# An expert FFN on one Trainium2 core: the first two up products before the last group's counts

## The reference

```python
gate = softmax(flat_x @ w_gate.T)                  # 8 experts
topk_scores, topk_idx = top_k(gate, 2)
cw = (one_hot(topk_idx, 8) * topk_scores[..., None]).sum(axis=1)
h = gelu(einsum('td,edh->teh', flat_x, W1) + b1, approximate=False)   # hidden width 512
y = einsum('teh,ehd->ted', h, W2) + b2
out = einsum('ted,te->td', y, cw)
```

## Time and profile before

| | us |
|---|---|
| median of 3 runs | 810.93 |
| lowest, highest | 807.05, 812.1 |
| profiled execution, its own time | 804.24 |
| its span, first to last instruction | 802.3 |
| TensorE matmuls busy | 417.3 (52%) |
| VectorE busy | 440.9 (55%) |
| ScalarE busy | 333.3 (42%) |
| GpSimd busy | 290.7 (36%) |
| mean granted clock of TensorE | 0.728 |

### The profile page before, as it was taken

The page is one execution under the profiler, slowest core; times in us unless marked ns, Lnnn a source line. Parts: engine busy times, 40 slices in busy tenths (PEclk is TensorE's granted clock), DMA queues, the critical chain, the costliest instruction groups (busy, mean ns, idle before and its releaser), DMA issues.

```text
span 802.3 us, 14898 instructions
## 1 busy us (share of the span) xinstructions
PE 417.3 (52%) x4184; PEld 348.2 (43%) x4185; DVE 440.9 (55%) x1035; ACT 333.3 (42%) x746; POOL 290.7 (36%) x344
## 2 busy tenths in 40 slices
PE   5444773400076500546299999211599935887000
PEld 4334662400065400435099998000498814675000
DVE  7888888301188501655078888010499914666713
ACT  3444884210187210443066765000366603456621
POOL 3281000777300575028600003777000172431773
PEclk9766886655588655668589999555699966798555
DMA  9940334211235211303134334221133322331622
GB/s 236 308 133 1 104 123 126 77 51 52 85 114 156 60 51 40 106 27 93 59 73 93 98 92 111 66 56 52 43 93 97 94 76 56 88 90 51 186 69 65
DMA packets 129680, 73.19 MB, mean 91 GB/s; under 512 B 53744, under 2 KB 122992, under 8 KB 129392
## 3 DMA queue, kind: packets, MB, share of 16 engines
q1 hardware_dynamic: 121456, 56.02, 25.5%
q0 software_dynamic: 8192, 16.79, 7.2%
HBM read 21.75 MB, written 34.90 MB: 71 GB/s over the span
## 4 chain that ended last, share of the span: by engine, by line
PE 40%; issue 28%; DVE 15%; another core or an unknown queue 5%; ACT 5%; POOL 4%; DVEq 1%; DMA 1%; ACTq 1%; SPq 0%; POOLq 0%
PE psA L1160 17%; PE psA L1148 8%; POOL ROW L493 4%; PE psV L1148 4%; PE psH L1148 4%; DVE ATT L753 2%; PE psH L1057 2%; DVE stats L692 2%; PE psA L1066 1%; DVE w_bound L928 1%; PE psA L1068 1%; DVE X L825 1%; PE psA L1067 1%; ACT ATT L589 1%
## 5 line engine op out<-in xcount | busy, mean ns | idle before, releaser
L493 POOL DMA_INDIRECT ROW<-slot_out,POS x128 | 131.6, 1028 | 259.7 <-DMA slot_out<-VP 166.7
L482 POOL DMA_INDIRECT slot_rows<-ROW,POS x128 | 127.7, 998 | 194.1 <-DVE EXPT L903 156.0
L1160 PE MATMUL psA<-WST,ATT 128*128 x2040 | 155.9, 227 | 68.7 <-issue 66.6
L1160 PEld LDWEIGHTS psA<-WST,ATT 128*128 128x128 f16 x2040 | 132.2, 101 | 90.1 <-issue 82.9
L967 DVE TENSOR_SCALAR ATT<-ATT,f_scales 128x1024 f16<-128x1024 f32 x85 | 63.9, 752 | 166.4 <-remote 133.1
L637 ACT ACTIVATE ATT<-psA,b1T,f_scales 128x256 f32<-128x256 f32 x172 | 83.0, 562 | 141.2 <-issue 63.8
L969 DVE SCALAR_TENSOR_TENSOR ATT<-ATT,f_scales 128x1024 f16<-128x1024 f32 x85 | 109.1, 1284 | 3.0
L1148 PE MATMUL psA<-WT,WST 128*128 128x256 f16 x516 | 72.0, 287 | 12.6 <-issue 7.8
L637 ACT ACTIVATE ATT<-psV,b1T,f_scales 128x256 f32<-128x256 f32 x84 | 42.8, 560 | 75.1 <-PE psH L1148 49.2
L1057 PE MATMUL psH<-ident,ATT 128*128 128x128 f32 x64 | 15.1, 379 | 94.2 <-DVE ATT L753 76.5
L1148 PEld LDWEIGHTS psA<-WT,WST 128*128 x516 | 49.8, 102 | 24.8 <-issue 17.4
(11 more groups left out here) (197 smaller groups left out, 723.7 us busy)
## 6 DMA issues: line engine op xcount, KB each, us to landing
slot_out<-VP SPq DMA_DIRECT2D x85, 128.0 KB
slot_rows<-zero SPq DMA_DIRECT2D x9, 1024.0 KB, 5.4
X<-in_x SPq DMA_DIRECT2D x8, 512.0 KB, 7.0
WST<-in_W SPq DMA_DIRECT2D x2, 2048.0 KB, 14.9
WST<-WT SPq DMA_DIRECT2D x16, 256.0 KB
out<-X SPq DMA_DIRECT2D x16, 256.0 KB
slot_rows<-ROW,POS POOLq DMA_INDIRECT x128
GA<-gate_rows SPq DMA_DIRECT2D x1, 2048.0 KB, 9.6
```

What stands on the lines that cost most here:

```text
L482: nc.gpsimd.indirect_dma_start(xg[g], bass.IndirectOffsetOnAxis(ap=POS[:, k * TILES + t:k * TILES + t + 1], axis=0), ROW[:, t * 2 * D:(t + ...
L493: nc.gpsimd.indirect_dma_start(YG[:, o:o + D], None, yg[g], bass.IndirectOffsetOnAxis(ap=POS[:, i:i + 1], axis=0)).then_inc(gathered[c % 2 ...
L1160: last = mm(psD[k % 2][:, h * D:(h + 1) * D], a[:, k % 2, i:i + TOK], W2S[:, ds(e * 2 * FF + b * FF + m * D, D)], start=(m == 0 and c == 0 ...
```

## The change

TensorE's part of `route(2)` is taken out of its place and its two counting matmuls, now in `count`, stand between slot 1's and slot 2's up products. Slot 0's and slot 1's up products stand ahead of them, right behind the attention part. The counts go to bank X, whose readers are done by `hT_ready`, so that bank V and H are free for slot 1. The wait for the row copies stands between slot 0 and slot 1. The wait for `rbase_link` goes. ScalarE's, VectorE's, GpSimd's and SyncE's programs keep their order; VectorE reads the counts from the other bank.

```diff
 def ffn_loop(eng, stages, mix=None, between=None):
...
+                    if between:
+                        between(k)
...
             fetch(0, 0)
-            turn(0)
+            turn(0, between=between)
...
+        def rank_banks(g):
+
+            n = GT[g] * E
+            return (psX[:, 0:n], psX[:, 256:256 + n]) if g == GROUPS - 1 else (psV[:, 0:n], psH[:, 0:n])
...
+                ranks, totals = rank_banks(g)
...
-                link(nc.vector.tensor_tensor_scan(flat(8), notfirst[:, E * first:E * (first + gt)], psH[:, 0:n], 0.0, ALU.mult, ALU.add))
+                link(nc.vector.tensor_tensor_scan(flat(8), notfirst[:, E * first:E * (first + gt)], totals, 0.0, ALU.mult, ALU.add))
...
-                tt(te(11), psV[:, 0:n].rearrange("p (t e) -> p t e", e=E), turned(10), ALU.add).then_inc(rbase_link, 1)
+                tt(te(11), ranks.rearrange("p (t e) -> p t e", e=E), turned(10), ALU.add).then_inc(rbase_link, 1)
...
+            def count(g):
+
+                n = GT[g] * E
+                ranks, totals = rank_banks(g)
                 pe.wait_ge(route_const, GROUPS + 1)
                 pe.wait_ge(choice_ready, g + 1)
-                pe.wait_ge(vp_ready, min(PAIRS, PAIRS_TO[g] + 2))
-                pe.wait_ge(row_ready, PAIRS_TO[g])
...
+                mm(ranks, upper[:], RC16[:, 0:n], start=True, stop=True)
+                mm(totals.rearrange("p (e t) -> p e t", e=E), onesh[:], RC16[:, 0:n].rearrange("p (t e) -> p e t", e=E),
                    start=True, stop=True).then_inc(rank_done, 1)
-                pe.wait_ge(rbase_link, g + 1)
+
+            def route(g):
+
+                if g < GROUPS - 1:
+                    pe.wait_ge(vp_ready, min(PAIRS, PAIRS_TO[g] + 2))
+                    pe.wait_ge(row_ready, PAIRS_TO[g])
+                    count(g)
+                    pe.wait_ge(rbase_link, g + 1)
...
-            pe.wait_ge(row_ready, PAIRS)
             pe.wait_ge(pos_ready, 1)
             pe.wait_ge(t2_ready, PAIRS)
-            ffn_loop(pe, ((0, up, True), (-2, down, True)))
+            pe.wait_ge(hT_ready, PAIRS)
+
+            def between(k):
+
+                if k == 0:
+                    pe.wait_ge(vp_ready, PAIRS)
+                    pe.wait_ge(row_ready, PAIRS)
+                if k == 1:
+                    count(GROUPS - 1)
+
+            ffn_loop(pe, ((0, up, True), (-2, down, True)), between=between)
```

More of the change, by code:

```diff
@@ L251, in steps, with ffn_loop @@
             route(GROUPS - 1)
-        def ffn_loop(eng, stages, mix=None):
+        def ffn_loop(eng, stages, mix=None, between=None):
             offsets = [d for d, _, needs in stages if needs]
@@ L267, in fetch, with turn @@
                     eng.load(held[lo:lo + count], EXPT[0:1, ds(BODY * n + lo, count)])
-            def turn(n, steps=BODY, mix=None):
+            def turn(n, steps=BODY, mix=None, between=None):
                 static = isinstance(n, int)
@@ L1125, in step @@
                     last.then_inc(mem_done, 1)
-            def route(g):
+            def count(g):
+                n = GT[g] * E
+                ranks, totals = rank_banks(g)
                 pe.wait_ge(route_const, GROUPS + 1)
                 pe.wait_ge(choice_ready, g + 1)
-                pe.wait_ge(vp_ready, min(PAIRS, PAIRS_TO[g] + 2))
-                pe.wait_ge(row_ready, PAIRS_TO[g])
-                n = GT[g] * E
-                mm(psV[:, 0:n], upper[:], RC16[:, 0:n], start=True, stop=True)
-                mm(psH[:, 0:n].rearrange("p (e t) -> p e t", e=E), onesh[:], RC16[:, 0:n].rearrange("p (t e) -> p e t", e=E),
-                   start=True, stop=True).then_inc(rank_done, 1)
-                pe.wait_ge(rbase_link, g + 1)
+                mm(ranks, upper[:], RC16[:, 0:n], start=True, stop=True)
+                mm(totals.rearrange("p (e t) -> p e t", e=E), onesh[:], RC16[:, 0:n].rearrange("p (t e) -> p e t", e=E),
+                   start=True, stop=True).then_inc(rank_done, 1)
+            def route(g):
[4 more added lines that the diff above has]
+                    pe.wait_ge(rbase_link, g + 1)
             steps(pe, step, route, {-1: first_gates})
```

## The result

The change made the kernel slower: 814.14 us against 810.88 us, 20 runs each, ratio 1.0036 with a 95% interval of 1.0022 to 1.0051. That is +3.3 us between the medians where I had forecast -1.5. A second sample gave 1.0013 (0.9989 to 1.0038), whose interval holds 1, and a third 1.0032 (1.0015 to 1.0050).

What follows compares the result with a forecast made beforehand. The prediction took TensorE's starved instruction flow during GpSimd's indirect-DMA bursts as the bound, then the seam. A lead of -2.5 us plus 1.0 for the clock gave -1.5, so 809.4 us against 810.93, range 801 to 817.

Steps and rivals of the forecast that it cites:

- the law: Expert loop: TensorE's instructions starve during each GpSimd burst of indirect DMAs, after a delay of 18.3, 7.7 or 4 us.
- The seam: Stretch from 344 to 360 between attention and expert loop, where TensorE, VectorE and ScalarE wait; the change edits it.
- My lead of 2.5 us: First down product of slot 0 starts at 357.6 instead of 360.11.
- the wait of the counts behind slot 1: Counting matmuls queue behind slot 1's up product: 1.2 to 2.0 us late, taken as 1.7, delaying route and scatter.
- The clock: TensorE idles before the first down product and may drop to the low clock: cost 0 to 2.2 us, 1.0 taken.
- GpSimd beside VectorE: First three scatters of group 2 now run beside VectorE's splits: up to 2.9 us longer; counted 0 to +1, 0 taken.
- it sets in at the same distance from the burst's start: Group 2's scatter: the starved stretch moves 1.7 us later with the scatter and keeps its 29.4 us.
- rival 1: Group 2's scatter: TensorE, already primed, starves sooner; +5.1 us (816.0) or +7.0 (817.9); chance 0.27.
- one of the signs that I had named for being wrong: Profile: an onset of starvation that moves against the scatter's start by more than 3 us.
- Rival 2: Group 2's scatter: starvation comes after an amount of TensorE work, eating the lead; -0.3 us, 810.6; chance 0.20.
- Rival 3: Group 2's scatter: busy VectorE slows GpSimd, so starvation sets in much later; -7.5 us, 803.4; chance 0.11.
- Rival 4: Seam: the change doesn't do what it says, for example rows not landed at 344.9; 812.6 at most; chance 0.02.

Runs made afterwards that it cites:

- e7: Kernel before, with each of group 2's scatters waiting for one more up product (one per slot): 781.47 us, ratio 0.9609.
- e8: Changed kernel with one scatter of group 2 per slot, a repeat run beside the equally paced kernel before: 776.96 us, ratio 0.9571.
- e12: Changed kernel with one scatter of group 2 per slot, plus 60 unused matmuls ahead of the first down product: 769.29 us, ratio 0.9566.
- e5: The kernel before, unchanged, run and profiled a second time: ratio 1.0011 (0.9986 to 1.0035).
- e15: The kernel before, unchanged, run and profiled a third time: ratio 0.9998 (0.9972 to 1.0024).
- e3: Changed kernel, but GpSimd starts group 2's scatter only when the eighth down product is done: 818.29 us, ratio 1.0086.
- e13: Kernel before with group 2's counts in bank X at their old place in TensorE's queue, repeated with more rounds: 811.92 us, ratio 1.0006.
- e19: Changed kernel, but VectorE's first split is held until GpSimd has issued three scatters of group 2: 811.47 us, ratio 1.0004.
- e2: Changed kernel with the counts one slot earlier, between slot 0's and slot 1's up products, in bank X: 812.89 us, ratio 1.0016.
- e14: Changed kernel with only slot 0's up product ahead of the counts, which keep the old banks V and H: 813.0 us, ratio 1.0009.
- e1: Kernel before with group 2's counts in bank X and the wait for its readers, old place in TensorE's queue: 812.55 us, ratio 1.0035.
- e4: Changed kernel with each of group 2's scatters waiting for one more up product (one per slot), first run: 776.8 us, ratio 0.9576.
- the paced pair: Kernel before (e7) and changed kernel (e8), both with one scatter of group 2 per slot: 781.47 and 776.96 us.

## Why the prediction was wrong

**The order of the views, and the law.** "TensorE's instruction flow starves during a GpSimd burst, and comes back after it" held and carried everything. Spacing group 2's scatter takes 30 us off the kernel before (e7 against before on the same chip), 34 us together with the change (e8), and spacing the gathers beside the loop as well makes it 113 us.

**The seam.** My lead of 2.5 us was 4.2. The term that was off is the wait of the counts behind slot 1, which I took as 1.7 us: it is 0.0. I had slot 1 at the low clock, ending at 349.9 by the trace of before. But the granted clock rose between them, from 0.52 in 347.8 to 350.3 (slot 0) to 1.00 in 350.3 to 351.8 (slot 1), and slot 1's 12 matmuls took 1.5 us instead of 2.53. Slot 0 also followed the last transpose by 0.1 us and not by 0.83. The scatter starts 10.1 us behind the routing's start in both kernels.

**The clock.** Taken as 1.0 of 0 to 2.2; measured 1.7 (e8 against e12), and 1.7, after against before, between the first down product and the 97th product. The Trainium skill ("TensorE: Matmul & The Clock Gate", "Why this matters for your kernels") had it right, and I gave it half: TensorE waited for 3.97 us, the granted clock fell from 1.00 to 0.50 behind it, and the next 24 matmuls took 2.52 us. Lead and clock together were 2.6 us ahead, where my sum had 1.5.

**GpSimd beside VectorE.** The first three scatters took 0.96, 1.61 and 1.68 us instead of 0.96 each, 1.4 us more, within the bound of 2.9. But the whole burst got shorter, 42.0 us against 44.5 (43.7 and 44.7 in e5 and e15). The burst's length goes with the onset: 41.2 us in e3, where starvation began at 2.1, and 46.1 in e13, where it began at 26.4. A starved TensorE leaves VectorE little to do, and beside an idle VectorE a scatter takes 0.96 us. I had taken zero for the sum of these.

**The step that failed** is "it sets in at the same distance from the burst's start". The onset moved from 15.9, 16.4 and 16.2 to 9.3, 9.4 and 9.1: rival 1, and one of the signs that I had named for being wrong. The starved stretch, forecast at 29.4 us, took 36.1. Rival 1's price was written as +5.1 us against before for an onset 7.7 us in by eye; at 10.6 us by eye, the measured place of the 1201st product is 2.9 us behind. Its sum also comes out with measured terms, as an estimate: 63 products fewer by the break (125 against 188) are 4.9 us at 152 in 11.9 us, less 2.4 us of a shorter burst, +2.5.

That the starved stretch took the gain back is shown: with it the change costs 3.3 us, without it (e7 and e8) it saves 3.5 to 4.5. Why the onset moved is shown only in part. Rival 1's reason, a stream that is already primed when the burst comes, is borne out by e3 and e19. Where the stream was in full flow before the burst, the onset came at 2.1 us; where it started 2.2 us into the burst (after and e2), at 9.1 to 9.7; 5.9 us into it (e19), at 14.2; 6.5 us into it (before), at 15.9 to 16.4. But e14, with a start 2.6 us in, has 6.1, and e1 and e13, one program with the start of before, have 9.7 and 26.4. So the start of the stream against the burst moves the onset in most of these profiles and doesn't fix it. I had given this rival 0.27, less than the forecast, on the ground that the bursts with a short onset were gathers; e3's is a scatter and has the shortest.

Rival 2, that the onset comes after an amount of TensorE's work, is excluded: beside the burst TensorE did 89 products by the break (357.30 to 367.90), against 179 before. Rival 3, a later onset, too. Rival 4 didn't come true: slot 0's first matmul ran 0.1 us behind the last transpose. The median moved by 3.3 us, and the profiles account for 2.9 at the end of the scatter; the last product is 3.9 behind in the means of three (401.9 against 398.0), and the 1.0 between these lies in the gather bursts and within their spread.

**The profile of before.** Its time of 804.24 us stands outside all that the first three runs gave, as I wrote, and its seam was typical of the program, as I assumed. So both terms of it could be used; the time's difference between the two first profiles (9.6 us) could not.

**What stays open.** No run shows what it is in a GpSimd burst that stops TensorE's instructions, nor why e1 and e13, one program, had onsets of 9.7 and 26.4. Before and after have three profiles each, and every other kernel here has one (two for e1's program, and two for e4's, e4 and e8). With a spread like that of e1 and e13, the onsets of e2, e3, e14 and e19 are single draws.

## What to carry to other kernels

A stretch whose length isn't set by the work you speed up, here a starved one that hangs on another engine's burst, can take back a gain that was real: measure the edit once with that stretch removed (the paced pair: -4.5 us between medians) before judging it. Where an engine starves beside another's burst of transfers, spacing the burst over the work it hides behind can be worth far more than a reordering at its edge: two waits brought 113 us here, some 4 us of them from the change. And where an effect of 3 us is asked for in a kernel whose executions spread by 9, one profile of each side can mislead: e1 looked like proof of the wrong cause.

## What the runs showed of the hardware that I had not expected

- 30 indirect transfers one per slot (40 us of GpSimd) beside a full stream cost TensorE nothing (93.0 of 93.0 us busy); in close order TensorE did 31 matmuls in 36.1 us. Two per slot cost 18% of the matmuls while they lasted.
- The time that TensorE lasts against a burst was 2.1 us with the stream in full flow at the burst's start, and 9.3, 14.2 and 16 us with a stream that started 2.2, 5.9 and 6.5 us into it. It isn't fixed by this: 9.7 and 26.4 us in two executions of one program.
- The granted clock stood at 1.00 through a wait of 3.9 us and fell to 0.50 only behind it, while TensorE was at work again. That cost 1.7 us. With 60 matmuls that nobody uses in the wait, it stayed at 1.00.
- No packet of an instruction queue lies in the starved stretch of the gathers.
- The counting matmuls in a bank of their own, read by VectorE there, take the same time as in the old banks (0.27 and 0.41 us in before and in e1).
